# Two turns at a time at the end of a graph kernel, and two more rows finished by GpSimd

## The chip, the cores and the metric
One core of one Trainium2 chip. The metric is the device time of the whole kernel in microseconds (us); smaller is better. Times inside the kernel are counted from the start of the profiled span.

## The reference, cut to what matters
A graph of 8192 nodes with 64 features and a dense adjacency matrix `adj` of 8192 x 8192 in fp32. Layer 0 is a Chebyshev filter of order 3, layer 1 a hyperbolic one:

```
h = relu(layernorm(x))
T1 = adj @ h;  T2 = 2*(adj @ T1) - h;  T3 = 2*(adj @ T2) - T1
x = x + h@W0 + T1@W1 + T2@W2 + T3@W3 + bias0
h = relu(layernorm(x));  p = tanh(|h|) * h/|h|      (norm clipped to 10)
s = adj @ p                                          (level 4)
x = x + (arctanh(|s|) * s/|s|) @ kernel + bias1      (norm clipped to 0.999)
```

Four products with the matrix follow each other; the kernel calls them levels 1 to 4.

## The kernel before, in words
The matrix is cut into 16 x 16 blocks of 512 x 512 (1 MB each, row r, column c). A *visit* multiplies one block on TensorE with the features of column c. The planner `work_order()` writes out one list of steps by hand, and every engine walks through the same list in its own queue, taking the steps that concern it and waiting on semaphores. SyncE's queue loads the blocks into a ring of 13 slots (L613), in the order of the visits that need them, and at the end issues one store for each row of 512 nodes (L622), in the order of the batches.

At the end of the list stands level 4. The visits `("AGAIN", r, 15, 4)` of column 15 come last: (15,15), (0,15), (1,15), ... (14,15), each completing one row. A visit (`by_node_halves`, L690, recorded on tiles of 128x32) makes 32 recorded matmul instructions and writes work bank 0 or 1 by turns. VectorE adds the bank to the row's sum (L1105).

When the row is complete, `complete(row, 4)` sets a countdown of visits after which the step `TURN` stands in the list. TURN of a row on TensorE (`to_nodes`, L703, tiles of 64x64, 16 recorded instructions) multiplies the finished sum with the identity and with the last weight, into one of three pairs of banks used in rotation. It waits for VectorE's addition for that row, and for the evacuation of the turn three before. Behind TURN:

- ScalarE squares one half of the result (L972) and copies the other half (L973).
- `SQUARES`: VectorE sums the squares (L1265).
- After four turns, `RADIUS`: ScalarE takes a root (L977) and loads the table for the logarithm (L978); VectorE makes a chain of short operations on 128x16 (L1275 to L1294).
- With the next turn, or at the end of the list, `LOGS` (ScalarE, L982 and L983, then the table load back to the root, L986, except in the last batch) and `RESULT` (VectorE, L1300 to L1302: the ratio). Then each row of the batch gets one multiplication by the ratio and one addition to the residual, either on GpSimd (L661, L664) or on VectorE (L1309, L1313).

The batches are (15,0,1,2), (3,4,5,6), (7,8,9,10), (11,12,13,14). `by_vector` and `by_pool` say who finishes which row. SyncE waits for each row in this order before it issues its store. In the kernel before, the order around turn 11 is: visit (12,15), TURN 11, SQUARES 11, LOGS, RESULT of rows 7 to 10, visit (13,15), TURN 12, SQUARES 12, visit (14,15), TURN 13, SQUARES 13, TURN 14, SQUARES 14, RADIUS, LOGS, RESULT.

```
batches = [s[1:] for s in steps if s[0] == "RESULT"]
by_vector = [*batches[-2][:2], *batches[-1][1:]]      # rows 7, 8, 12, 13, 14
by_pool = [r for rows in batches for r in rows if r not in by_vector]
```

Of the kernel before, what the change touches and what calls it, by code (L numbers as in the profile page):

```python
# [12 lines left out]
def work_order():  # L13
# [11 lines left out]
    def follow(n, step, then):  # L25
        countdown.append([n, step, then])

    def one_visit_passed():
        for c in countdown:
            c[0] -= 1  # L30
        while any(c[0] <= 0 for c in countdown):
            c = next(c for c in countdown if c[0] <= 0)
            countdown.remove(c)
            steps.extend([c[1]] if c[1] else [])
            c[2]()

    def complete(row, level, visits_to_turn=2):
        if level < 4:
            steps.append(("SUM", row, level))

        def known_now():
            known.add((level + 1, row))
            if level == 1:
                follow(3, None, lambda: known.add(("SUMS", row)))

        def norm():
            follow(2, ("NORM", row), scale)

        def scale():
            follow(2, ("SCALE", row), expand)  # L50

        def expand():
            follow(1, ("EXPAND", row), lambda: follow(1, None, known_now))

        if level == 1 and row == NB - 1:
            visits_to_turn = 3
        if level == 2 and row < FAST_BELOW:
            follow(1, ("JOIN", row, 2, 0), lambda: None)
            visits_to_turn = 4
        if level == 3 and row >= FAST_FROM:  # L60
            follow(2 if row < NB - 1 else 1, ("JOIN", row, 3, 0), lambda: None)
            visits_to_turn = 5 if row < NB - 1 else 4
        follow(visits_to_turn, ("TURN", row, level), norm if level == 3 else known_now)
# [7 lines left out]
    def both_columns(row):  # L71
        if sweep[0] == 0:
            return range(min(row, NB - 2))
        if sweep[0] == 1:
            return range(max(row + 1, LOW), NB) if row < HIGH else range(0)
        return range(row if LATE_FROM <= row < NB - 1 else row - 1) if row > LOW else range(0)

    def row_complete(row, level):
        both = all((sweep[0], "BOTH", row, c) in done for c in both_columns(row))
        if level == 1:  # L80
            joined = all(g in steps for g in joins_of.get(row, []))
            return both and joined and all((0, "FRESH", row, c) in done for c in fresh_columns(row))
        if level == 2 and row >= HIGH:
            return all((0, "AGAIN", row, c) in done for c in range(min(row, NB - 2), NB))
        if level == 4:
            return all((2, "AGAIN", row, c) in done for c in range(row, NB))
        return both and (level == 2 or all((2, "OWN", row, c) in done for c in own_columns(row)))

    def visit(kind, row, col, *level):
        steps.append((kind, row, col) + level)  # L90
        done.add((sweep[0], kind, row, col))
        if kind == "BOTH" and (row, col) in group_ends and sweep[0] == 0:
            n = group_ends[row, col]
            steps.append(("SWAP", row, 1, n))
            follow(2, ("JOIN", row, 1, n), lambda: row_complete(row, 1) and complete(row, 1))
        elif kind == "BOTH" and sweep[0] > 0 and is_fast(row, sweep[0] + 1):
            if all((sweep[0], "BOTH", row, c) in done for c in both_columns(row)):
                steps.append(("SWAP", row, sweep[0] + 1, 0))
        if kind == "AGAIN":
            if sweep[0] == 0 and row >= HIGH and row_complete(row, 2):  # L100
                complete(row, 2)
            if sweep[0] == 2 and row_complete(row, 4):
                complete(row, 4)
        elif row_complete(row, sweep[0] + 1):
            complete(row, sweep[0] + 1, 3 if (sweep[0], row) == (2, LOW) else 2)
        one_visit_passed()
# [26 lines left out]
    for j in range(NB):  # L133
        visit("FRESH", 0, j)
        if j % 2 == 0 and j + 5 < NB:
            steps.append(("H", j // 2 + 3))
        if 2 <= j:
            steps.append(("H_TURN", j - 2))
        if 3 <= j < NB - 1:
            steps.append(("H_TERM", j - 3))  # L140
# [12 lines left out]
    while rows or blocks:  # L153
        (b0, f0), (b1, f1) = next((g for g in zip(goals, goals[1:]) if g[1][0] > both_done), (goals[-2], goals[-1]))
        due = f0 + (f1 - f0) * (both_done + 1 - b0) / (b1 - b0)
        may_fresh = rows and (rows[0][1] < 2 or ("SUM", rows[0][1] - 2, 1) in steps) and             (rows[0][1] < NB - 1 or not blocks)
        may_both = blocks and next_is_known(blocks) and (blocks[0][1] < PANELS[0] or ("SUMS", blocks[0][2]) in known)
        if again and next_is_known(again) and ("SUMS", again[0][1]) in known:
            visit(*again.pop(0))
        elif may_both and (fresh_done >= due or not may_fresh):  # L160
            visit(*blocks.pop(0))
            both_done += 1
        elif may_fresh:
            visit(*rows.pop(0))
            fresh_done += 1
        else:
            visit(*blocks.pop(0))
            both_done += 1
        if left:
            steps.append(left.pop(0))  # L170
# [73 lines left out]
def is_fast(row, level):  # L244

    return level == 1 and row >= PANELS[0] or level == 2 and row < FAST_BELOW or level == 3 and row >= FAST_FROM
# [37 lines left out]
def chebyshev_hyperbolic_kernel(nc, x, adj_blocks, cheb_weight, cheb_bias, hyp_kernel, hyp_bias, out):  # L284
# [175 lines left out]
    batches = [s[1:] for s in steps if s[0] == "RESULT"]  # L460
    place = {r: (b, n) for b, rows in enumerate(batches) for n, r in enumerate(rows)}

    by_vector = [*batches[-2][:2], *batches[-1][1:]]
    by_pool = [r for rows in batches for r in rows if r not in by_vector]


# [873 lines left out]
```

How the kernel before makes its waits and increments, by code:

```python
        @block.sync  # L598
        def _(sp):
            def load_x(g):
                rows = slice(H_GROUPS[g][0] * C, (H_GROUPS[g][-1] + 1) * C)
                sp.dma_start(resid[:, rows, :], x[:, rows, :]).then_inc(s_x[g], 16)
            for n in range(loads):
                r, c = steps[first_step_of[n]][1:3]
                if n == 0:
                    load_x(0)
                    load_x(1)
                if n + 2 < len(H_GROUPS):
                    load_x(n + 2)
                if freed_by[n]:
                    sp.wait_ge(s_visit, freed_by[n])
                sp.dma_start(ring[:, slot_of[n], :, :], adj_blocks[(r * NB + c) * P:(r * NB + c + 1) * P, :, :])\
                    .then_inc(s_landed[slot_of[n]], 16)
            for s in steps:
                if s[0] == "RESULT":
                    for r in s[1:]:
                        if r in by_pool:
                            sp.wait_ge(s_pooled, by_pool.index(r) + 1)
                        else:
                            sp.wait_ge(s_result, by_vector.index(r) + 1)
                        sp.dma_start(out[:, chunks(r), :], resid[:, chunks(r), :]).then_inc(s_out, 16)
            sp.wait_ge(s_out, NB * 16)
# [1 line left out]
        @block.gpsimd  # L625
        def _(pool):
            nc.gpsimd.memset(ident[:, :], 0.0).then_inc(s_zeroed, 1)
            pool.wait_ge(s_zeroed, 1)
            nc.gpsimd.affine_select(out=ident[:, :], in_=ident[:, :], compare_op=ALU.not_equal, fill=1.0,
```

## Time and profile before

| | |
|---|---|
| median of 3 runs | 1758.21 us (1756.56 to 1758.4) |
| profiled execution, its own time | 1759.25 us |
| its span | 1757.2 us |
| TensorE matmul busy | 1710.1 us (97%) |
| VectorE busy | 1287.5 us (73%) |
| ScalarE busy | 266.9 us (15%) |
| GpSimd busy | 163.2 us (9%) |
| DMA, mean over the span | 379 GB/s |
| chain that ended last, by engine | TensorE 79%, DMA 13%, VectorE 6% |

Busy time is the time in which the engine had an instruction in work; the chain is what, step by step, released the instruction that ended last. The profiled execution's own time is larger than its span, since the span runs from the first to the last instruction. PE is TensorE's matmul, PEld its weight load, DVE VectorE, ACT ScalarE, POOL GpSimd, SPq the queue of SyncE.

### The profile page before, as it was taken

How to read it: one execution, taken by the hardware profiler on the slowest of the kernel's cores; microseconds unless marked ns; L12 is line 12 of the kernel's file. 1: busy time of each engine (PE TensorE's matmuls, PEld its weight loads, DVE VectorE, ACT ScalarE, POOL GpSimd, SP SyncE). 2: the span in 40 equal slices, each digit the busy share in tenths (PEclk: the TensorE clock that was granted, in tenths of full speed). 3: DMA queues.
4: the chain of work that ended last, by engine and by line, in shares of the span. 5: the costliest groups of instructions: out<-in, count | busy, mean ns of one | idle time of the engine just before them, and what ended most of it. 6: DMA issues, size and time to landing. Idle time of an engine off the chain costs nothing.

```text
span 1757.2 us, 66874 instructions
## 1 busy us (share of the span) xinstructions
PE 1710.1 (97%) x30828; PEld 1017.0 (58%) x30828; DVE 1287.5 (73%) x2104; ACT 266.9 (15%) x507; POOL 163.2 (9%) x224
## 2 busy tenths in 40 slices
PE   7999999999999999999999999999999999999997
PEld 5655555555566555555555665566655555655554
DVE  7157777776778697689898886487778776776756
ACT  1013122111111011011100001222111101010014
POOL 0000000000000110211001000111001001000003
PEclk9999999999999999999999999999999999999999
DMA  9999999999999988888998987799999999999996
GB/s 364 420 420 418 418 419 416 412 415 406 404 410 406 391 306 294 313 324 330 338 341 333 341 327 288 265 386 399 402 419 410 407 420 415 419 419 411 418 419 276
DMA packets 95014, 665.14 MB, mean 379 GB/s; under 512 B 11408, under 2 KB 13712, under 8 KB 14608
## 3 DMA queue, kind: packets, MB, share of 16 engines
q1 hardware_dynamic: 93744, 660.64, 94.2%
q8 instruction: 243, 3.98, 0.9%
q10 hardware_dynamic: 992, 0.23, 0.1%
q14 instruction: 35, 0.29, 0.0%
HBM read 658.74 MB, written 2.10 MB: 376 GB/s over the span
## 4 chain that ended last, share of the span: by engine, by line
PE 79%; DMA 13%; DVE 6%; issue 1%; SPq 1%; ACT 0%; POOL 0%; DVEq 0%; ACTq 0%
PE own_bank L788 22%; PE row_bank L788 18%; DMA ring<-adj_blocks 13%; PE work_bank L690 12%; PE row_bank L690 9%; PE work_bank L788 7%; PE turned L690 5%; PE turned L703 1%; DVE ring L1069 1%; PE row_bank L826 1%; PE work_bank L804 1%; PE own_bank L690 1%; DVE ring L1073 1%; PE own_bank L804 1%; PE row_bank L804 0%
## 5 line engine op out<-in xcount | busy, mean ns | idle before, releaser
L1069 DVE TENSOR_TENSOR ring<-ring 128x1024 f32<-128x1024 f32 x323 | 401.7, 1244 | 131.2 <-DMA ring<-adj_blocks 62.6
L788 PE MATMUL own_bank<-ring 128*32 128x256 f32 x5024 | 432.0, 379 | 0.2
L788 PE MATMUL own_bank<-ring,nodes 128*32 128x256 f32 x3768 | 384.7, 379 | 1.2 <-DVE ring L1069 1.0
L788 PE MATMUL row_bank<-ring 128*32 128x256 f32 x3488 | 300.2, 379 | 0.0
L788 PEld LDWEIGHTS own_bank<-ring 128*32 128x32 f32 x5024 | 230.6, 110 | 108.7 <-DVE ring L1073 1.6
L690 PE MATMUL row_bank<-ring,nodes 128*32 128x256 f32 (+1 forms) x3856 | 266.0, 382 | 18.0 <-DMA ring<-adj_blocks 17.3
L788 PE MATMUL row_bank<-ring,nodes 128*32 128x256 f32 x2616 | 266.4, 379 | 3.7 <-POOL ring L649 1.9
L690 PE MATMUL work_bank<-ring,nodes 128*32 128x256 f32 x4288 | 252.6, 380 | 4.6 <-DVE acc L1026 1.5
L788 PEld LDWEIGHTS own_bank<-ring,nodes 128*32 128x32 f32 x3768 | 189.9, 110 | 84.0 <-DVE ring L1069 4.5
L1075 DVE TENSOR_TENSOR ring<-ring 128x512 f32<-128x512 f32 x323 | 230.2, 713 | 11.0
L1073 DVE TENSOR_TENSOR ring<-ring 128x512 f32<-128x512 f32 x323 | 229.1, 709 | 11.1
L690 PEld LDWEIGHTS row_bank<-ring,nodes 128*32 128x32 f32 (+1 forms) x3856 | 143.9, 114 | 118.4 <-DMA ring<-adj_blocks 27.2
L788 PEld LDWEIGHTS row_bank<-ring 128*32 128x32 f32 x3488 | 161.5, 110 | 74.5
L690 PEld LDWEIGHTS work_bank<-ring,nodes 128*32 128x32 f32 x4288 | 139.0, 110 | 96.1 <-issue 10.9
L788 PEld LDWEIGHTS row_bank<-ring,nodes 128*32 128x32 f32 x2616 | 132.3, 110 | 60.8 <-DVE ring L1069 3.2
L788 PE MATMUL work_bank<-ring 128*32 128x256 f32 x1824 | 155.4, 379 | 0.0
L788 PE MATMUL work_bank<-ring,nodes 128*32 128x256 f32 x1368 | 142.9, 380 | 0.2 <-issue 0.2
L1105 DVE TENSOR_TENSOR partial<-partial,work_bank 128x256 f32<-128x256 f32 x104 | 43.6, 419 | 107.0 <-PE work_bank L690 106.6
L644 POOL TENSOR_TENSOR ring<-nodes 128x128 f32<-128x128 f32 x41 | 27.0, 658 | 931.3 <-DVE nodes L1217 610.4
L788 PEld LDWEIGHTS work_bank<-ring 128*32 128x32 f32 x1824 | 83.3, 110 | 39.3
L690 PE MATMUL turned<-ring,nodes 128*32 128x256 f32 (+1 forms) x1712 | 103.7, 379 | 0.4 <-DMA ring<-adj_blocks 0.4
L788 PEld LDWEIGHTS work_bank<-ring,nodes 128*32 128x32 f32 x1368 | 69.2, 110 | 30.7 <-issue 1.6
(165 smaller groups left out, 1159.1 us busy)
## 6 DMA issues: line engine op xcount, KB each, us to landing
ring<-adj_blocks SPq DMA_DIRECT2D x626, 1024.0 KB, 10.5
out<-resid SPq DMA_DIRECT2D x16, 128.0 KB, 4.2
resid<-x SPq DMA_DIRECT2D x7, 256.0 KB, 11.9
resid<-x SPq DMA_DIRECT2D x2, 128.0 KB, 3.8
w_raw<-cheb_weight ACTq DMA_DIRECT2D x2, 64.0 KB, 8.7
bias<-cheb_bias ACTq DMA_DIRECT2D x1, 32.0 KB, 3.1
bias<-hyp_bias ACTq DMA_DIRECT2D x1, 32.0 KB, 5.4
w_raw<-hyp_kernel ACTq DMA_DIRECT2D x2, 16.0 KB, 9.7
```

The source lines that it names most:

```text
L644: nc.gpsimd.tensor_tensor(s1, features(c, 1, 0), features(c, 1, 1), ALU.add)
L690: done = nc.tensor.matmul(bank[lane:lane + size, N1], nodes[:, c * C + k, level, part:part + size], data[:, k, half * 2 * P:(half + 1) * 2 ...
L703: done = nc.tensor.matmul(pair[lane:lane + TURN_SIZE, half, to:to + width], source[rows, at:at + TURN_SIZE], weight[rows, :], start=k == 0 ...
L788: done = nc.tensor.matmul(bank[lane:lane + H, columns], left(a, h, level), right[b][:, h, :], start=first and k < 2, stop=k == 6, tile_pos ...
L804: done = nc.tensor.matmul(to[lane:lane + H, columns], nodes[:, c * C + k, lane // F, part:part + H], data[:, k, columns], start=to is bank ...
L826: done = nc.tensor.matmul(bank[lane:lane + size, :], nodes[:, c * C + k, lane // F, lane % F:lane % F + size], data[:, k, :], start=first ...
L1069: nc.vector.tensor_tensor(first_two(n, block), block[:, :, N2].rearrange("p (k h) n -> p k h n", k=2), block[:, 0:2, :].rearrange("p h (k ...
L1073: nc.vector.tensor_tensor(mix_of(n, 1), block[:, 2:4, N2], mix_of(n, 0), ALU.subtract).then_inc(s_mixed, 1)
L1075: nc.vector.tensor_tensor(mix_of(n, 2), block[:, 2:4, N1], mix_of(n, 1), ALU.subtract).then_inc(s_mixed, 1)
L1105: done = nc.vector.tensor_tensor(partial[:, r, N1], partial[:, r, N1], bank[:, N1], ALU.add)
```

## The change
Turns of level 4 are put in pairs: the countdown of an odd row is 3 visits, that of an even row stays 2. The list then has two visits, then two turns, down to the end: visits (0,15), (1,15), TURN 15, TURN 0, visits (2,15), (3,15), TURN 1, TURN 2, and so on. Around turn 11 it becomes: visits (12,15), (13,15), TURN 11, SQUARES 11, LOGS, RESULT of rows 7 to 10, TURN 12, SQUARES 12, visit (14,15), TURN 13, SQUARES 13, TURN 14, SQUARES 14, RADIUS, LOGS, RESULT. RADIUS of rows 7 to 10 stands before the addition of visit (12,15), as before. The work banks, the ring slots and the order of the loads stay as they were. And rows 7 and 8 go from VectorE to GpSimd, which then finishes all of 7, 8, 9, 10 and, as before, row 11.

```
--- before.py
+++ after.py
@@ -100,7 +100,7 @@
             if sweep[0] == 0 and row >= HIGH and row_complete(row, 2):
                 complete(row, 2)
             if sweep[0] == 2 and row_complete(row, 4):
-                complete(row, 4)
+                complete(row, 4, 3 if row % 2 else 2)
         elif row_complete(row, sweep[0] + 1):
             complete(row, sweep[0] + 1, 3 if (sweep[0], row) == (2, LOW) else 2)
         one_visit_passed()
@@ -460,7 +460,7 @@
     batches = [s[1:] for s in steps if s[0] == "RESULT"]
     place = {r: (b, n) for b, rows in enumerate(batches) for n, r in enumerate(rows)}
 
-    by_vector = [*batches[-2][:2], *batches[-1][1:]]
+    by_vector = list(batches[-1][1:])
     by_pool = [r for rows in batches for r in rows if r not in by_vector]
```

## Rows read from the trace of the kernel before

**Rows 1.** Stretches of the end: start:end, length, busy (instructions), granted clock, DMA, GB/s

```profile
1690.00:1704.50 14.50, 13.04 (x244) 7.46 (x236) 7.28 (x23) 3.63 (x7) 0.73 (x1) 1.00 1.01 419
...
1725.20:1743.40 18.20, 18.20 (x340) 9.87 (x336) 10.93 (x54) 11.19 (x28) 8.54 (x14) 1.00 0.83 332
...
1746.00:1757.20 11.20, 1.16 (x32) 0.84 (x27) 6.57 (x27) 3.12 (x9) 2.63 (x3) 0.76 0.25 83
```

**Rows 2.** Timeline of TensorE's visits (L690) and turns (L703): start, length, instructions

```profile
1706.26 3.66 PE L690 MATMUL work_bank<-ring,nodes 128*32 128x256 f32 x64
...
1709.85 0.67 PE L703 MATMUL turned<-turn,partial 64*64 64x128 f32 x16
...
1710.45 1.93 PE L690 MATMUL work_bank<-ring,nodes 128*32 128x256 f32 x32
...
1712.31 0.67 PE L703 MATMUL own_bank<-turn,partial 64*64 64x128 f32 x16
...
1725.22 2.52 PE L690 MATMUL work_bank<-ring,nodes 128*32 128x256 f32 x32
...
1738.15 2.31 PE L690 MATMUL work_bank<-ring,nodes 128*32 128x256 f32 x32
```

**Rows 3.** The load of block (13,15) by its line: issue, and time to landing

```profile
L613 SPq DMA_DIRECT2D ring<-adj_blocks x1: 5313/5313/5313, 1710.2 to 1710.2; - x1
...
DMA to landing us min/median/max: 29.5/29.5/29.5
```

**Rows 4.** Timeline of all engines from turn 11 to the square of row 14

```profile
1740.39 0.67 PE L703 MATMUL turned<-turn,partial 64*64 64x128 f32 x16
...
1741.12 0.38 ACT L972 ACTIVATE tmp<-turned 128x256 f32<-128x256 f32 x1 [0.24 <-PE turned L703]
...
1741.77 0.21 ACT L983 ACTIVATE radii<-radii 128x16 f32<-128x16 f32 x1
...
1742.26 0.16 DVE L1300 TENSOR_TENSOR radii<-radii 128x16 f32<-128x16 f32 x1
...
1742.92 1.12 POOL L661 TENSOR_TENSOR nodes<-nodes,radii 128x256 f32<-128x256 f32 x1 [4.31 <-DVE radii L1302]
...
1743.59 0.38 ACT L972 ACTIVATE tmp<-own_bank 128x256 f32<-128x256 f32 x1
...
1745.44 0.40 DVE L1265 TENSOR_REDUCE radii<-tmp 128x4 f32<-128x256 f32 x1
...
1745.77 0.40 DVE L1105 TENSOR_TENSOR partial<-partial,work_bank 128x256 f32<-128x256 f32 x1
...
1746.45 0.70 PE L703 MATMUL turned<-turn,partial 64*64 64x128 f32 x16
...
1747.30 0.39 ACT L972 ACTIVATE tmp<-turned 128x256 f32<-128x256 f32 x1
```

**Rows 5.** Timeline of GpSimd: the first and the last of its eight instructions for batch 0

```profile
1722.61 0.61 POOL L661 TENSOR_TENSOR nodes<-nodes,radii 128x256 f32<-128x256 f32 x1 [21.16 <-DVE radii L1302]
...
1727.44 0.73 POOL L664 TENSOR_TENSOR resid<-resid,nodes 128x256 f32<-128x256 f32 x1
```

**Rows 6.** A meeting of GpSimd and VectorE, and VectorE's line (min/median/max in ns)

```profile
1096.44 0.73 POOL L653 TENSOR_TENSOR resid<-resid,bias 128x256 f32<-128x256 f32 x1 [3.51 <-DVE squares L1239]
1096.47 0.72 DVE L1248 TENSOR_TENSOR small<-roots,small 128x4 f32<-128x4 f32 x1
...
L1248 DVE TENSOR_TENSOR small<-roots,small x16: 161/161/717, 1096.5 to 1701.7; 128x4 f32<-128x4 f32 x16
```

**Rows 7.** Timeline of the last batch: RADIUS on VectorE, row 11 on GpSimd, the stores

```profile
1748.39 0.17 DVE L1276 TENSOR_TENSOR radii<-radii 128x16 f32<-128x16 f32 x1
...
1748.76 0.17 DVE L1279 SCALAR_TENSOR_TENSOR radii<-radii 128x16 f32<-128x16 f32 x1
...
1751.28 1.38 POOL L661 TENSOR_TENSOR nodes<-nodes,radii 128x256 f32<-128x256 f32 x1 [4.82 <-DVE radii L1302]
...
1753.55 1.79 SPq L622 DMA_DIRECT2D out<-resid  x4
```

More of the change, by code:

```diff
@@ L102, in visit @@
             if sweep[0] == 2 and row_complete(row, 4):
-                complete(row, 4)
+                complete(row, 4, 3 if row % 2 else 2)
         elif row_complete(row, sweep[0] + 1):
@@ L461, in chebyshev_hyperbolic_kernel @@
     place = {r: (b, n) for b, rows in enumerate(batches) for n, r in enumerate(rows)}
-    by_vector = [*batches[-2][:2], *batches[-1][1:]]
+    by_vector = list(batches[-1][1:])
     by_pool = [r for rows in batches for r in rows if r not in by_vector]
```

## The prediction

> **What bounds the kernel now.** The table of stretches comes first [rows 1]. From 1690 to 1704.5 us TensorE is busy 13.0 of 14.5 us with the DMA engines full: transfers set the pace. From 1725.2 to 1743.4 it is never idle, and DMA has thinned to 0.83. After 1746 only 1.2 us of matmul are left in 11.2 us: a tail of short VectorE and ScalarE steps, GpSimd and stores. The change touches nothing before the visit of block (1,15), at about 1710 us, so at most the last 48 us can move.
>
> The second view is the timeline of TensorE [rows 2]. Two visits in a row start 1.73 us apart (64 instructions; the turn starts at 1709.85, 3.59 after the first visit: 1.73 and 1.86). A turn starts 1.86 after its visit, and the next visit 0.60 after the turn. So each visit with its turn takes 2.46 us. Going between the two tile shapes costs 0.13 on the way in and at most 0.17 on the way out.
>
> The third view is the landing of the blocks [rows 3]: (13,15) is issued at 1710.2 and lands 29.5 later, at 1739.7. That is only 1.3 us ahead of its use: the visit starts at 1740.99 (turn of row 11 at 1740.39, plus 0.60) [rows 4]. A block of 1.05 MB at 419 GB/s [rows 1] takes 2.5 us, as long as TensorE takes to use it. **A faster TensorE meets the DMA after about one microsecond.**
>
> The fourth is the timeline of all engines over turns 11 to 14 [rows 4]. The multiplications and additions of rows 7 and 8 by VectorE come just after the ratio (GpSimd starts on it at 1742.92) and keep VectorE until about 1745.2. Hence row 14's last addition starts at 1745.77, and turn 14 at 1746.45.
>
> **The change part by part.** *Pairs.* Seven pairs of turns arise: (15,0), (1,2), ... (11,12); 13 and 14 stand together already. No instruction is added on TensorE. Each pair saves one change of shape in and one out: 0.13 at least, 0.30 at most, so 0.9 to 2.1 us over seven. A turn after a turn is not in the trace with both ready; its bounds are 0.43 (0.60 less the 0.17) and 0.60.
>
> How much arrives? Row (1,15) could start at 1706.26 + 2 x 1.73 = 1709.72. From there to (13,15) are six pairs of 1.86 + (0.43 to 0.60) + 0.60 + 1.73 = 4.62 to 4.79, and the two visits that were long (2.52 and 2.31 for 1.93 [rows 2]) add 0.59 and 0.38: 1738.4 to 1739.4. The block lands at 1739.7. I take V = 1739.8 for its start, 1.2 us earlier than before. DMA decides that, at either bound.
>
> *What is late next.* Pairing also moves work in ScalarE's queue. Before, turn 11 was evacuated, then came LOGS with its table load, while TensorE made visit (13,15), and turn 12 was ready just as ScalarE was. Now turn 12 is done half a microsecond after turn 11, but its evacuation waits behind LOGS and the load. VectorE's SQUARES of row 12 waits for that, row 14's last addition is queued behind SQUARES, and turn 14 waits for the addition. By rows [rows 4], from V:
> turn 11 at V + 1.86 = 1741.66; its square on ScalarE 0.73 later (1740.39 to 1741.12), 1742.4; the square of row 12 another 2.47 later (1741.12 to 1743.59), 1744.87; SQUARES of 12 after 0.41 (0.38 and a step across), 1745.28; row 14's addition 0.33 later (1745.44 to 1745.77), 1745.61; turn 14 0.68 later (1745.77 to 1746.45), 1746.29; its square 0.73 to 0.85 later, 1747.02 to 1747.14. Before it was 1747.30. **Of 1.2 us gained at V, 0.2 us is left.** (14,15) itself starts near 1742.7 and does not bind.
>
> *Rows 7 and 8 by GpSimd.* VectorE loses one multiplication of 128x512 and two additions, some 2.3 us. That would have freed row 14's addition, but the chain above now holds it at nearly the same time; so no gain over the kernel before is to be had from it beyond that 0.2 us. Without it, the pairs' ratio would start 2.3 us of VectorE at about 1743.9, SQUARES of row 12 would come at 1746.2 and the addition at 1746.5, 0.9 us later: with the pairs alone the end would be later than this sum by so much, less the collision below. GpSimd gets four rows in place of two. The ratio: the log ends 0.86 after the square of row 11, VectorE's three steps and the handover take 0.66 (1742.26 to 1742.92), so GpSimd starts at about 1743.94 instead of 1742.92. Four rows take 4.83 to the start of the eighth instruction and 0.73 for it [rows 5], so it ends at 1749.50. Row 11 is only wanted near 1751.2 [rows 7], so GpSimd is free for it. The stores of rows 7 to 10 are issued before that too, so the four that SyncE issues from 1753.55 stand behind nothing new.
>
> *A collision the trace before has in no RADIUS stage.* RADIUS of the last batch has its first two-input instruction at 1748.39 [rows 7], now 0.2 earlier: 1748.19. GpSimd's seventh instruction then runs from 1748.08 to 1748.69 and its eighth from 1748.77 to 1749.50. What such a meeting costs stands in [rows 6]: a 128x4 VectorE operation with two SBUF inputs, started 0.03 after a GpSimd addition of 0.73, took 0.72, as long as GpSimd; the median of its 16 is 0.16. So L1276 ends with the seventh, at about 1748.71 instead of 1748.36 (+0.35); L1279, 0.20 after that, ends with the eighth, at 1749.52 instead of 1749.08 (+0.44). Sum: +0.8 us. Bounds: none, if neither meets, and +1.3, if a third instruction is caught. Nothing hides this: RADIUS, RESULT and the four stores that are issued one behind the other from 1753.55 [rows 7] are one chain.
>
> The Trainium skill (SBUF — State Buffer, Who interferes with whom) says that the shared port pair is an exclusive lock held for a whole instruction, and that tensor_scalar in its two-port mode takes it too. On the first the row agrees (0.72 beside 0.73). The second no row shows; by it L1277 and L1278, between the two, would also stop, and the collision would cost about 1.1 instead of 0.8.
>
> The same overlap, about 0.9 us, arises between batch 0 on GpSimd (1723.5 to 1729.1) and RADIUS of batch 1 (about 1728.2). It costs VectorE some 0.6 us, and then row 8's addition; TensorE waits for the DMA there anyway.
>
> **Sum.** -0.2 + 0.8 = +0.6 us: span 1757.2 to 1757.8. The profiled execution took 1759.25, 2.05 more than its span, and 1.04 more than the median of the runs, 1758.21. So its own time would be 1759.8, and the median 1758.8.
>
> **Rivals.** *The pairs' gain arrives* (faster): no collision, and the addition of row 14 isn't held by ScalarE. Turn 14 would come at V + 1.86 + 1.03 + 1.86 + 0.14 + 0.42 + 0.28 = V + 5.6 = 1745.4, 1.05 earlier: 1757.2. With the hold but no collision: 1758.0. For it: the collision hangs on tenths. Against it: the order of the queues is fixed, and GpSimd's end and the start of RADIUS both hang on V, so that a shift of V doesn't part them.
> *V is not earlier*: stores of batch 0 and the collision in RADIUS 1 push loads or turn 8, and (13,15) starts at 1741.0 as before. All behind it comes 1.2 later: 1760.0. Against it: slack of 0.3 us or more in every pair by the bounds above.
> *The clock falls* (slower by over 0.2%): TensorE now waits some 0.1 to 0.4 us in each pair for a block. If the granted clock went from 2.4 to 1.2 GHz, a visit would take 3.46 us; two visits so (+3.5 us) are where it decides, and six pairs would cost 21 us: 1779. Against it: 1.5 us idle in 14.5 left it at 1.00, and 0.76 is seen only with 1.2 us of work in 11.2 [rows 1].
> *The pairs don't arise*: excluded, the countdown of visits to a turn is 3 for odd rows and 2 for even ones.
>
> **How the numbers follow.** Collision and hold, +0.1 to +1.1: 0.6, predicted 1758.8 (its own range 1758.2 to 1759.4). Gain arrives wholly or in part: 0.22. V not earlier: 0.16. Clock: 0.02. Runs of before lie between 1756.56 and 1758.4, the profiled one at 1759.25, so a median may sit 0.6 us off. The range 1756.8 to 1760.3 holds the first three. A change of 0.2%, 3.5 us, is what a measurement can tell from none; only the clock exceeds it above, nothing here reaches it below. With what the runs scatter: faster 0.02, same 0.95, slower 0.03.
>
> **What the profile after would show.** Pairs: 64 visit instructions in one row and 32 turn instructions in another. DMA bound: the second visit of a pair idle before its start on the block; (13,15) at 1739.8. Hold: square of row 12 right after the load, row 14's addition at about 1745.6. Collision: L1276 or L1279 at 0.4 to 0.7 us in the last batch instead of 0.17, GpSimd busy until 1749.5. The prediction is wrong if (13,15) starts elsewhere, if L1276 and L1279 keep 0.17, or if GpSimd is late for row 11.

## The result, and the profile after

The changed kernel takes 1760.35 us, the median of 17 runs (1759.1 to 1761.92), against 1757.97 us for the kernel before, the median of 17 runs beside them (1756.56 to 1758.68). The ratio is 1.0015 with a 95% interval of [1.0008, 1.0022]: 2.4 us slower, clear of no change, and below the 0.2% named in the prediction. The forecast was 1758.8 with a range up to 1760.3; the measured time lies just above the range. The profiled execution of the changed kernel took 1759.74 us with a span of 1757.7.

The stretches of the end of the changed kernel, in the same columns as [rows 1]:

```profile
1690.00:1704.50 14.50, 13.57 (x256) 8.11 (x252) 7.08 (x22) 3.19 (x5) 0.73 (x1) 1.00 1.01 419
1725.20:1743.40 18.20, 16.79 (x338) 10.05 (x340) 10.91 (x53) 9.90 (x27) 7.38 (x12) 1.00 0.76 303
1746.00:1757.70 11.70, 0.57 (x16) 0.32 (x15) 7.08 (x25) 2.68 (x7) 5.33 (x7) 0.66 0.27 90
```

The clock stays at 1.00 until the tail, so that rival is out. In the second stretch TensorE is now idle 1.4 us where it had no idle time before, and GpSimd works 5.3 us in the last stretch instead of 2.6.

The timeline of TensorE in the changed kernel (PEld is its weight load), which answers [rows 2]:

```profile
1709.68 0.67 PE L703 MATMUL turned<-turn,partial 64*64 64x128 f32 x16
1710.07 0.48 PEld L703 LDWEIGHTS own_bank<-turn,partial 64*64 64x64 f32 x16
1710.17 0.62 PE L703 MATMUL own_bank<-turn,partial 64*64 64x128 f32 x16
...
1710.72 1.93 PE L690 MATMUL work_bank<-ring,nodes 128*32 128x256 f32 x32
...
1712.82 1.93 PE L690 MATMUL work_bank<-ring,nodes 128*32 128x256 f32 x32 [0.16 <-DMA ring<-adj_blocks]
...
1729.98 0.67 PE L703 MATMUL row_bank<-turn,partial 64*64 64x128 f32 x16
...
1731.99 0.46 PEld L703 LDWEIGHTS turned<-turn,partial 64*64 64x64 f32 x16 [1.59 <-issue]
1732.03 0.67 PE L703 MATMUL turned<-turn,partial 64*64 64x128 f32 x16 [1.38 <-ACT nodes L973]
```

A turn behind a turn starts 0.49 us after it (1709.68 to 1710.17) and the visit 0.55 us after that: 1.04 for two, inside the forecast bounds of 1.03 to 1.20. Visit (3,15) waits for its block, as forecast: it starts 0.14 us after the landing. Visits (5,15) and (7,15) do the same, the later second visits of a pair do not. Not forecast is the last pair of rows: turn 8 starts 2.05 us after turn 7.

The end of the changed kernel, from the table load of LOGS to the last RADIUS, which answers [rows 4] and [rows 7]:

```profile
1743.10 1.28 ACT L986 ACT_TABLE_LOAD   x1
...
1744.50 0.36 ACT L972 ACTIVATE tmp<-own_bank 128x256 f32<-128x256 f32 x1
...
1744.90 0.42 DVE L1265 TENSOR_REDUCE radii<-tmp 128x4 f32<-128x256 f32 x1 [1.20 <-ACT tmp L972]
...
1745.23 0.41 DVE L1105 TENSOR_TENSOR partial<-partial,work_bank 128x256 f32<-128x256 f32 x1
...
1745.90 0.67 PE L703 MATMUL turned<-turn,partial 64*64 64x128 f32 x16 [0.85 <-DVE partial L1105]
...
1747.22 0.72 POOL L664 TENSOR_TENSOR resid<-resid,nodes 128x256 f32<-128x256 f32 x1
...
1747.49 0.48 DVE L1275 TENSOR_SCALAR radii<-radii 128x16 f32<-128x16 f32 x1
...
1747.90 0.61 POOL L661 TENSOR_TENSOR nodes<-nodes,radii 128x256 f32<-128x256 f32 x1
1748.01 0.54 DVE L1276 TENSOR_TENSOR radii<-radii 128x16 f32<-128x16 f32 x1
...
1748.60 0.72 POOL L664 TENSOR_TENSOR resid<-resid,nodes 128x256 f32<-128x256 f32 x1
1748.74 0.61 DVE L1279 SCALAR_TENSOR_TENSOR radii<-radii 128x16 f32<-128x16 f32 x1
```

The first half is the hold: table load, square of row 12, SQUARES, row 14's addition, turn 14, each at once behind the other. The second half is the collision: L1276 ends within 0.04 us of GpSimd's seventh instruction and L1279 of its eighth. A third was caught too, L1275, a tensor_scalar that took 0.48 instead of 0.17 and ended 0.03 after the sixth (1747.22 to 1747.94).

**Where the 2.4 us are.** Two executions can be compared only from a common point, because everything ahead of it scatters: in two profiles of the kernel before, visit (15,15) starts at 1706.26 and at 1703.85, and from there to the end they take 50.96 and 51.06 us. So all profiles are cut at the start of (15,15). From the starts of the visits and turns in each trace; each column counts from the event of the column before it, "time" is the difference of the timed medians from before:

```
kernel, profile            (13,15) (14,15) turn 14 the end    sum   time
before, first                34.73    2.46    3.00   10.76  50.96
before, second               35.06    2.46    2.79   10.75  51.06   -0.4 (no difference)
changed, first               35.08    3.07    3.38   11.78  53.32   +2.4
changed, second              34.58    3.07    3.39   11.79  52.83   +2.7
pairs only                   35.23    3.07    4.45   10.68  53.43   +2.3
GpSimd only                  34.45    2.46    3.13   11.10  51.15   -0.4 (no difference)
row 7 single                 35.02    3.07    3.38   11.77  53.25   +2.0
LOGS later                   34.92    3.42    2.68   12.21  53.23   +2.1
LOGS later, row 10 vector    35.32    3.53    3.41   11.38  53.64   +2.3
row 10 vector                37.40    3.07    3.38   11.04  54.90   +1.2
pairs early                  36.00    2.46    2.67   11.10  52.23   +1.5
pairs late                   33.69    3.15    3.31   11.79  51.93   +1.5
row 11 single                36.44    2.46    2.68   11.23  52.81   +1.4
rows 7 to 10 left out        34.40    3.07    3.39   10.71  51.57   +1.4
two pairs                    35.04    2.46    3.54   10.78  51.82   +0.8
two pairs, row 10 vector     34.94    2.46    2.68   10.64  50.72   -0.3 (no difference)
changed, 64 ahead            36.17    2.96    3.30   11.78  54.21   +1.4
changed, 128 ahead           35.58    4.02    3.25   11.78  54.63   +2.2
before, 64 ahead             36.10    2.46    3.36   10.64  52.56   +0.9
before, 128 ahead            37.29    2.46    3.36   10.64  53.76   +1.6
```

The last column is from 11 runs of the kernel (17 in the first comparison) and 17 to 33 of before; its interval is some 1.2 to 1.6 us either side. So differences of about 1 us between two of these versions are not shown by the times alone; what separates them is the columns of the traces, each from a single execution. The two need not agree: the profiled execution of row 10 vector took 1.7 us more than the median of its kernel, that of 128 ahead 1.5 and 1.0 more.

Two cautions in reading it. With the pair (11,12), turn 11 stands behind (13,15) and no longer ahead of it, so the second column is 0.6 us longer (3.07 for 2.46) by the order alone. And in those unshifted kernels the start of (13,15), taken as the 33rd matmul of a row of 64, lies some 0.2 us early: turn 11 starts 2.04 after it, where 1.86 is usual. The start of (14,15) has neither fault, since in both orders it stands behind the same visits and turns.

Before to changed, as means of two profiles: to (14,15) 37.35 to 37.90, +0.55, where the forecast had it sooner; on to turn 14 2.90 to 3.39, +0.49; to the end 10.76 to 11.79, +1.03. Together +2.1 of the 2.4 us.

Up to (14,15) the sums can be made from the steps read above (1.73, 1.86 and 0.60 in [rows 2], 0.49 and 0.55 with pairs). Before, a stream without a stop would need 36.2 us, changed 34.1: seven pairs give 2.0. On top came 1.0 and 1.3 us before, 4.0 and 3.5 us changed. Of the 4.0, 1.04 are the waits of (3,15), (5,15) and (7,15) for their blocks, and 2.95 are three stops, in (7,15), between turns 7 and 8, and in (12,15). In the kernel before the two stops, in (7,15) and (12,15), are all of the 1.0.

### The profile page after: what moved, and what is told of

Its sections match the earlier page's. It is cut to its first block, busy times and chain, and to the rows that moved or that the text cites. A ratio compares the mean times of both kernels' runs of the same rounds, so it can differ in the third digit from the quotient of the medians.

```text
span 1757.7 us, 66877 instructions
## 1 busy us (share of the span) xinstructions
PE 1708.5 (97%) x30828; PEld 1023.2 (58%) x30828; DVE 1287.4 (73%) x2101; ACT 266.5 (15%) x507; POOL 165.1 (9%) x228
## 4 chain that ended last, share of the span: by engine, by line
PE 79%; DMA 13%; DVE 5%; issue 1%; SPq 1%; ACT 0%; POOL 0%; DVEq 0%; ACTq 0%
PE own_bank L788 22%; PE row_bank L788 18%; DMA ring<-adj_blocks 13%; PE work_bank L690 12%; PE row_bank L690 9%; PE work_bank L788 7%; PE turned L690 5%; PE turned L703 2%; DVE ring L1069 1%; PE row_bank L826 1%; PE work_bank L804 1%; PE own_bank L690 1%; DVE ring L1073 1%; PE own_bank L804 1%; PE row_bank L804 0%
## 5 line engine op out<-in xcount | busy, mean ns | idle before, releaser
L690 PE MATMUL row_bank<-ring,nodes 128*32 128x256 f32 (+1 forms) x3856 | 264.3, 382 | 17.1 <-DMA ring<-adj_blocks 16.5
L690 PE MATMUL work_bank<-ring,nodes 128*32 128x256 f32 x4288 | 252.1, 380 | 4.6 <-issue 3.1
L690 PEld LDWEIGHTS row_bank<-ring,nodes 128*32 128x32 f32 (+1 forms) x3856 | 144.5, 114 | 116.2 <-DMA ring<-adj_blocks 26.1
L690 PEld LDWEIGHTS work_bank<-ring,nodes 128*32 128x32 f32 x4288 | 140.0, 110 | 96.6 <-issue 11.2
L690 PE MATMUL turned<-ring,nodes 128*32 128x256 f32 (+1 forms) x1712 | 103.3, 379 | 0.6 <-DVE partial L1105 0.6
```

The lines of the kernel that those rows point to most:

```text
L690: done = nc.tensor.matmul(bank[lane:lane + size, N1], nodes[:, c * C + k, level, part:part + size], data[:, k, half * 2 * P:(half + 1) * 2 ...
```

## The experiments

**The kernel before and the changed one again.** No edit; two more profiles and new times.

> The kernel before, unchanged, as a second profile and a null comparison. Theory A (all of the change lies in the last 50 us; the profiled execution of before, 1759.25, was a high draw over its median 1757.97): ratio 1.000, the stretch from the turn of row 15 to the end again 47.3 to 47.7 us, the span some 1 us shorter than 1757.2, and the difference lies before that turn. Theory B (the tail itself varies from one execution to the next): the stretch differs from 47.5 by 1 us or more.

> The changed kernel again, as a second profile. Theory A: time +2 to +2.5 us as before, stretch from the turn of row 15 to the end 48.0 us within 0.3, of which the last RADIUS again holds a collision of about 1.1 us with GpSimd. Theory B (the tail varies, by a wait of TensorE between turns 7 and 8 that was 1.4 us in the first profile): that wait is another length or is gone, and the stretch moves with it.

Before: 1757.39 us against 1757.79, ratio 0.9999 [0.9990, 1.0008]. The span was 1754.9, and the 2.3 us less than in the first profile lie ahead of (15,15). Changed: 1760.45, ratio 1.0015 [1.0006, 1.0024]. The wait between turns 7 and 8 was there again (gap of 1.44 us, against 1.59), hold and collision too. My marker of the expectation, the turn of row 15, was badly chosen: pairing itself moves that turn behind visit (1,15). It made the tails look nearly alike (47.4 and 48.0); the table above uses visit (15,15).

**Each part alone.**

```
pairs only:    by_vector = [*batches[-2][:2], *batches[-1][1:]]     # as before
GpSimd only:   complete(row, 4)                                     # as before
```

> Pairs alone, rows 7 and 8 stay on VectorE. Theory A: no meeting of GpSimd with the last RADIUS (about -1.1 us against the changed kernel), but VectorE has some 2.3 us of rows 7 and 8 after the ratio, so the addition of row 14 comes 0.9 us later; in sum 0.2 to 0.3 us below the changed kernel, so +1.8 to +2.3 us over before. Rival: the collision is the whole loss, then it equals the kernel before within 0.5 us.

> GpSimd finishes rows 7 and 8, turns stay single. Theory A: the addition of row 14 comes 0.3 us and turn 14 some 0.4 us earlier, and RADIUS of the last batch meets GpSimd's last two instructions, +0.5 to +0.9 us: in sum 0 to +0.5 us over before. Rival (the loss is made by GpSimd's rows alone): +2 us or more over before.

Pairs only: 1760.07, +2.3 us, ratio 1.0014 [1.0005, 1.0022]. GpSimd only: 1757.37, -0.4 us, ratio 0.9997 [0.9989, 1.0006], no difference. The times are as expected, with GpSimd only 0.4 us under the range. But there turn 14 came 3.13 us after (14,15), against 2.90 in the mean of before, and not 0.4 sooner, and the collision, by the last segment, was 0.3 us and not 0.5 to 0.9. With pairs only the last segment is 10.68, but turn 14 comes 7.52 us after (13,15), 4.45 after (14,15), since VectorE's 2.3 us of rows 7 and 8 now stand behind the late ratio. So the loss comes with the pairs; the GpSimd part trades 1.1 us there for 1.1 us of collision.

**The place in TensorE's instruction stream.** The trace names ScalarE as what ended the stop before turn 8, but turn 8 needs only evacuations that were long done, and its addition had ended at 1730.37. Stops of this kind stand at the same count of weight loads and waits in TensorE's stream: at 31200, 31333 and 31467 in the changed kernel, at 31200 and 31467 in the kernel before. To move the stream against these places, tiny matmuls were put at the very start:

```
             for k in range(WARM_UP):
                 nc.tensor.matmul(turned[ODD, 0, 0:P], ident[:, 0:F], ident[:, :], start=True, stop=True)
+            for k in range(16):        # 32 for 128 instructions
+                nc.tensor.matmul(turned[ODD, 0, 0:4], ident[:, 0:F], ident[:, 0:4], start=True, stop=True)
```

> The changed kernel with 16 more tiny matmuls (64 TensorE instructions) at its start, while TensorE waits for its first data; outputs unchanged. Theory C (the stop of 1.4 to 1.7 us between turns 7 and 8 is a fetch of instructions: such stops stand 133 weight loads apart in TensorE's stream, at 31200, 31333 and 31467): the stop leaves that place, since the same step now stands 32 weight loads further on, and a stop shows at the 31433rd load of the old count, within turns 9 and 10. Theory W (turn 8 waits for an engine): the stop stays between turns 7 and 8, 1.4 us or more. Time: within 1 us of the changed kernel in either case, since one pair's stop takes the place of another's.

> The same with 32 tiny matmuls (128 instructions). Theory C: no stop between turns 7 and 8; stops at the old loads 31266 (visit (8,15)), 31400 (visit (11,15)) and 31534 (inside turn 11); (13,15) starts 1 us or more earlier from the start of (15,15) than the 34.6 to 35.1 us of the changed kernel. Theory W: the stop stays and (13,15) with it.

> The kernel before with the same 128 instructions ahead, as the control for both: theory C says that its stops (0.46 at load 31201, 0.3 to 0.6 at load 31467) move to other steps and the time stays within 1 us of before. If it moved by more, shifts alone would explain the loss.

> The kernel before with 64 TensorE instructions (16 tiny matmuls) ahead, the control for the changed kernel with the same shift (1759.43 us). Fetch theory: its stops stand at the loads 31066, 31199, 31333 and 31465 of its own count, where the old stream had 32 loads less, and the time lies anywhere from 0 to 2 us above before (with 128 it was +1.6). Theory that pairs cost the same at any placement: then it lies 2.4 us below 1759.43, at 1757.0. If instead it lies within 1 us of 1759.43, most of the loss of the changed kernel at no shift is placement.

The weight loads of the changed kernel with 64 instructions ahead (L705 is the turn there), about turn 9:

```profile
1735.44 0.41 PEld L705 LDWEIGHTS own_bank<-turn,partial 64*64 64x64 f32 x12 [0.41 <-issue]
1737.14 0.20 PEld L705 LDWEIGHTS own_bank<-turn,partial 64*64 64x64 f32 x4 [1.29 <-issue]
```

The 1.29 us stop now stands inside one turn, between its twelfth and thirteenth weight load, where no semaphore is waited for. So no wait for another engine is needed for it. It is at the count 31465, as expected, and turn 8 starts 1.08 us after turn 7 instead of 2.05, held now by VectorE's addition; with 128 ahead the stop there is gone (0.49 us). Wherever such a stop stands at these places in the 20 profiles, the stream went on 2.3 to 2.7 us after the start of a 16 KB transfer on the instruction queue (q8 in the profile, 243 transfers in the whole kernel). In the changed kernel that transfer started at 1729.18 and TensorE ran dry at 1730.27; in the kernel before it started at 1729.64 and TensorE got there at 1732.07. The Trainium skill (Advanced Engine Details and Errata, ISA Cache) gives 16 KB, 256 instructions, as the line of the instruction cache; 133 loads and waits with the matmuls of the loads, 255 to 258 instructions, fit that.

The times: changed kernel +2.4 (no shift), +1.4 (64; ratio 1.0007 [0.9998, 1.0016]), +2.2 (128; 1.0014 [1.0005, 1.0022]). Kernel before: 0, +0.9 (64; 1758.79 us, 1.0004 [0.9995, 1.0013]), +1.6 (128; 1759.56 us, 1.0009 [1.0001, 1.0018]). So the placement alone moves the kernel before: by 1.6 us with 128 instructions ahead, just clear of no change; its 0.9 with 64 is not. I had expected at most 1 us for 128, and more was to mean that shifts alone can explain the loss; by that measure they can explain a good part. At equal shifts the changed kernel is 2.4, 0.6 and 0.6 us slower, and the two 0.6 are inside the interval. That pairing costs 2.4 us is shown for this placement, not for any. Nor can the cost of a placement be read from the last 50 us alone, since the shift moves the stops ahead of (15,15) too. The expectation of c2 that (13,15) would start 1 us sooner failed (35.58): other stops, of 1.2 us in visit (0,15) and about 0.9 us in two later places, stood ahead of it.

**The pair (7,8) taken apart.**

```
-                complete(row, 4, 3 if row % 2 else 2)
+                complete(row, 4, 3 if row % 2 and row != 7 else 2)
```

> The changed kernel with the one pair (7,8) taken apart: turn 7 after visit (8,15), turn 8 after visit (9,15). Fetch theory: the place 31333 of the stream now falls at the end of a visit, as in the kernel before, the stop of 1.3 us between turns 7 and 8 shrinks under 0.5, and (13,15) starts 0.5 to 1.2 us earlier from (15,15) (its block's landing is the limit): 0.5 to 1.0 us faster than the changed kernel. Rival (DMA alone holds (13,15)): no change in its start.

A miss: the stop before turn 8 stayed at 1.33 us and (13,15) at 35.02; 1759.95 us, ratio 1.0012 [1.0003, 1.0021]. The steps just before the place are now those of the kernel before, and still the transfer began only 0.95 us before TensorE got there. What happens next to the place doesn't decide; the pair (5,6), ahead of it, was still there.

**Early or late pairs.**

```
pairs early:  3 if row % 2 and (row < 7 or row == NB - 1) else 2
pairs late:   3 if row % 2 and 7 <= row < NB - 1 else 2
```

> The changed kernel with pairs only up to turns 5 and 6, single turns from row 7 on. GpSimd still finishes rows 7 to 10. If the early pairs are what keeps (13,15) from coming sooner (block waits and the late instruction fetch), (13,15) starts 34.5 to 35.2 us after (15,15) as in the changed kernel; turn 14 comes 5.5 us after it, not 6.45 (no hold), and from turn 14 to the end 11.1 us as with GpSimd alone: in sum 1.4 to 1.8 us below the changed kernel. If early pairs are harmless it is equal to before.

> The changed kernel with single turns up to row 6 and pairs from (7,8) on. If the loss before turn 14 is the hold alone, it keeps 6.45 us from (13,15) to turn 14 and 11.8 to the end, and equals the changed kernel within 0.5 us, whatever the early turns do. If (13,15) now comes 0.5 us or more sooner, the early pairs had delayed it.

Early: (13,15) at 36.00, later than the 34.5 to 35.2 expected, and the stop of 1.33 us is there. Late: (13,15) at 33.69, 1.2 us sooner than the mean of before (0.6 of it because turn 11 now stands behind it; (14,15) comes 0.5 us sooner), and the stop is gone; the transfer starts at 1728.96, and TensorE gets to the place 2.3 us later. Times 1759.18 (1.0007 [0.9998, 1.0016]) and 1759.14 (1.0008 [0.9999, 1.0017]), +1.5 for both. The weight loads of turn 8 with pairs late:

```profile
1731.67 0.46 PEld L703 LDWEIGHTS turned<-turn,partial 64*64 64x64 f32 x16 [0.28 <-issue]
```

So a gain ahead of (14,15) exists when the early turns are single, 0.5 us in this profile. With early pairs the transfer of instructions starts too late for the place 31333, and the stop eats it. All unshifted profiles divide in this way: in the ten with early pairs the stop at 31333 is 1.1 to 1.5 us, and the transfer starts 4.7 to 5.0 us after the stream went on at 31200; in the six with single early turns there is no stop above 0.2 us, and the transfer starts 3.8 to 4.0 us after that.

**The hold alone, in two ways.** First the pair (11,12) taken apart (`row != 11` in the condition); then LOGS and RESULT put behind the second turn of a pair:

```
-            out += [("SQUARES", s[1])] + waiting
-            waiting.clear()
+            out.append(("SQUARES", s[1]))
+            age += 1                      # set to 0 where RADIUS is put out
+            if age == 2:
+                out += waiting
+                waiting.clear()
```

> The changed kernel with only the pair (11,12) taken apart, so that turn 12's evacuation and the table load stand as before. Hold theory: turn 14 comes 5.3 to 5.6 us after (13,15) instead of 6.45, from turn 14 to the end 11.1 to 11.8 us: 0.9 to 1.6 us faster than the changed kernel. If the hold is not real: no change.

> The changed kernel with LOGS and RESULT of a batch moved behind the second turn of the next pair, so that the evacuation of turn 12 no longer stands behind the table load. Hold theory: turn 14 comes 5.4 us after the start of (13,15) instead of 6.45, but the ratio of rows 7 to 10 comes some 0.5 us later and RADIUS 1 us earlier, so RADIUS meets GpSimd for 1.5 us more and gives back most: -0.5 to +0.3 us against the changed kernel. If there is no hold, turn 14 stays at 6.4 and the time grows by the later ratio alone.

With row 11 single, turn 14 comes 5.14 us after (13,15) instead of 6.45; 1759.11 us, +1.4 over before in place of +2.4. Of these 1.3 us, 0.6 are turn 11, which stands ahead of (13,15) again. The hold is the rest, 0.7 us: from (14,15) to turn 14 2.68 instead of 3.39. The row of ScalarE that shows it, in that kernel:

```profile
1741.57 1.28 ACT L986 ACT_TABLE_LOAD   x1
...
1742.42 0.67 PE L703 MATMUL own_bank<-turn,partial 64*64 64x128 f32 x16
...
1742.87 0.20 ACT L986 ACTIVATE small<-ident 128x4 f32<-128x4 f32 x1
...
1743.15 0.38 ACT L972 ACTIVATE tmp<-own_bank 128x256 f32<-128x256 f32 x1
```

Turn 12 starts at 1742.42, the load ends at 1742.85: the load hides behind the visit. With LOGS later the hold is gone as well (2.68 from (14,15) to turn 14), but turn 14 comes 6.10 us after (13,15), not the 5.4 expected, since visit (14,15) itself starts later (3.42 us after (13,15), was 3.07). The later ratio lengthens the collision: 12.21 to the end. In sum 1759.99 us, 0.4 us below the changed kernel, inside the expectation.

**The collision alone, in three ways.** VectorE finishes row 10 (`by_vector = [batches[-2][3], *batches[-1][1:]]`); the same with LOGS later; and GpSimd leaves rows 7 to 10 out, with two memsets of 128x4 for each row in place of the multiplication and the addition.

> The changed kernel, but VectorE finishes row 10, so GpSimd has three rows of that batch. Collision theory (1.1 us of the loss is VectorE held by GpSimd in the last RADIUS): GpSimd ends at about 1747.2 on the changed kernel's clock, before RADIUS, L1275, L1276 and L1279 go back to 0.17; VectorE has some 1.2 us of row 10 before row 14's addition but waits there anyway for the square of row 12: in sum 0.8 to 1.1 us faster than the changed kernel, so +1.4 to +1.8 over before. If the collision costs nothing at the end, it equals the changed kernel.

> LOGS behind the second turn and row 10 finished by VectorE together, pairs kept. If hold and collision are both real and are the tail's loss, from turn 14 to the end it is 0.5 to 1 us shorter than with LOGS later alone, and the time is 1.0 to 1.8 us below the changed kernel. VectorE's 1.2 us of row 10 now stands right before row 14's addition, which takes up to 0.6 us of it back.

> The changed kernel, but GpSimd leaves out the multiplication and the addition of rows 7 to 10 (two tiny memsets stand in for them; their stored rows lack the second layer's term). Collision theory: L1275, L1276 and L1279 of the last batch take 0.17 us, from turn 14 to the end 10.7 us instead of 11.8, 0.9 to 1.2 us faster than the changed kernel. If the collision were hidden by something else at the end: no change.

With the rows left out: 1759.06 us, +1.4 in place of +2.4, and 10.71 us from turn 14 to the end instead of 11.78. Its RADIUS (L1283 is L1276 there):

```profile
1747.64 0.18 DVE L1282 TENSOR_SCALAR radii<-radii 128x16 f32<-128x16 f32 x1
1747.85 0.17 DVE L1283 TENSOR_TENSOR radii<-radii 128x16 f32<-128x16 f32 x1
```

The collision costs 1.1 us. With row 10 on VectorE the time was 1759.21, +1.2 (ratio 1.0007 [0.9998, 1.0016]), where 1.4 to 1.8 was expected; one instruction was still caught (0.58 us for L1276), and the last segment was 11.04. In this kernel's profile (13,15) stands at 37.40, as block (2,15) landed 1.4 us late and a stop of 1.67 us stood in visit (4,15). The combination missed: 1760.19, where 1 to 1.8 us below the changed kernel was expected. VectorE's work on row 10 now stands right before row 14's addition: 6.94 us to turn 14.

**A version without hold and collision.** Pairs (7,8) and (9,10) alone, `3 if row in (7, 9) else 2`, once with rows 7 and 8 and once with row 10 on VectorE.

> Pairs (7,8) and (9,10) alone, rows 7 and 8 on VectorE as in the kernel before: the part of the change that brought (13,15) forward, without hold and without collision. (13,15) starts 33.7 to 34.5 us after (15,15) (before 34.7 to 35.1), turn 14 5.2 to 5.5 us later, 10.7 to the end: 50 to 50.5 us instead of 51.0, that is 0.5 to 1 us faster than the kernel before. If (13,15) is not earlier, equal to before.

> The same two pairs, VectorE finishes row 10 alone and GpSimd rows 7 to 9: VectorE has 1.2 us less before row 14's addition (turn 14 5.14 us after (13,15)), and GpSimd ends before the last RADIUS or meets one instruction (10.7 to 11.1 us to the end). 0.3 us either side of the kernel with two pairs; if a meeting remains, 0.3 us slower than it.

Two pairs: 1758.61 us, +0.8, ratio 1.0005 [0.9996, 1.0013], not the gain expected, and not told from before; (13,15) did not come sooner (35.04), and VectorE's two rows held turn 14 for 6.00 us. With row 10 on VectorE: 1757.52 us against 1757.86, ratio 0.9999 [0.9990, 1.0008], 1.1 below the two pairs where 0.3 either side was expected. Its tail, 50.72 us, is the shortest in the table, but no difference from the kernel before can be told. No version here beats it.

## Why the prediction was right or wrong

- *What bounds.* As far as the profiles show, right: the tails from (15,15) hold 2.1 of the 2.4 us, and the pieces ahead scatter by 2.4 us between two profiles of one kernel.
- *The pairs on TensorE.* Right: a second turn costs 0.49 us, two turns and the way out 1.04, so seven pairs save 2.0 us, inside the forecast 0.9 to 2.1.
- *(13,15) starts 1.2 us sooner, since the DMA decides at either bound.* **This is the step that failed.** It started as late as before (34.83 against 34.90), although turn 11 no longer stood ahead of it; (14,15) came 0.5 us later than before. Its block had landed at 1738.4, a full 1.0 us before its start at 1739.44, so the DMA did not decide there. It decided only at (3,15), (5,15) and (7,15), 1.04 us together. I had taken the two long visits of [rows 2] as fixed additions of 0.59 and 0.38, 0.97 in all. They were stops for instructions, and their length depends on how late the transfer starts for the pace of TensorE. In the changed kernel there are three, and they add 2.95 us; read as gaps in the loads they are 0.62, 1.6 and 0.5. The rival "V is not earlier" with 1760.0 was given 0.16; it was the case, and nearest to the measured time, though by another cause than its own (stores and turn 8's addition). That its number fits is luck as far as the cause goes.
- *The hold by the table load.* Right in mechanism and near in size: from V to turn 14 6.49 us was forecast with the hold and 5.6 without it, 0.9 for the hold; 6.45 was measured, and 0.7 for the hold, by the kernels with row 11 single and with LOGS later.
- *Rows 7 and 8.* Right: by themselves no difference; with pairs only, turn 14 comes 7.52 us after (13,15), 1.07 later than with both, forecast 0.9.
- *The collision.* Right in mechanism for the last batch; 0.8 forecast, 1.0 to 1.1 measured. The missing part is L1275, the tensor_scalar, held from 1747.49 to 1747.97. The Trainium skill's sentence that this form can also take the pair (SBUF — State Buffer, Who interferes with whom) is borne out by this row. The 1.1 that I gave by that rule was the better figure, but by luck: the two that I named, L1277 and L1278, started at 1748.47 and 1748.55, about the gap between two GpSimd instructions, and took 0.16. The same overlap that I forecast for batch 1 did not come about: GpSimd ended at 1727.48, RADIUS began at 1727.51 and its steps took 0.17.
- *The sum.* With V unchanged, the forecast's own terms give 1.0 up to turn 14 and 0.8 for the collision, 1.8 us; measured 2.1 in the profiles and 2.4 in the times. The remaining 0.3 us is within the interval.
- *The base.* The profiled execution of before (1759.25) lay 1.3 us above the median of 17. Since only the difference was carried to the median, this cost nothing.

Open: why early pairs delay the start of the instruction transfer. Taking apart the pair next to the place changed nothing, taking apart all up to (5,6) removed the stop; what in between decides was not found. Open too is how much the change would cost averaged over placements.

## What to carry to other kernels

When TensorE gets a denser stream, ask what feeds it: data, and also instructions. A gap inside a run of equal instructions, or one whose named releaser does nothing that the next instruction needs, should be checked against the count of instructions, and a control with a few dummy instructions ahead shows how much of a small difference is placement. Before two steps are put side by side, look at what the other engines do between them: the table load was hidden exactly by the visit that pairing moved away. A row moved to an idle engine isn't free if that engine then works while short VectorE operations of the critical chain run: three of them took 0.3 to 0.4 us more each here.

## What the runs showed of the hardware

- TensorE stopped at fixed counts of its stream, about 133 weight loads and waits apart, until 2.3 to 2.7 us after a 16 KB transfer on the instruction queue had started. The transfers at these stops took 1.0 to 1.1 us themselves. The stops were 0 to 1.7 us. 128 cheap instructions at the start made the kernel before 1.6 us slower; with 64 the 0.9 us are not clear of no change.
- Three 128x16 VectorE operations that met a GpSimd one ended within 0.04 us of it: 0.48, 0.54 and 0.61 us instead of 0.17, a tensor_scalar among them.
